# Looked-up embedding rows put in place by SyncE's on-chip transfers of 16-byte pieces instead of ScalarE's copies

## The reference

```python
e = stack([tbl_f[ids[:, f]] for f in range(39)], axis=1)          # (1024, 39, 16)
def cin_layer(x0, xk, W, b):
    out = einsum('bhd,bmd,shm->bsd', xk, x0, W) + b[None, :, None]
    return relu(out)
x1 = cin_layer(e, e, W1, b1)                                       # (1024, 128, 16)
x2 = cin_layer(e, x1, W2, b2)
z = concatenate([x1.sum(axis=-1), x2.sum(axis=-1)], axis=-1)
h = concatenate([z, dense_ctx], axis=1)
h = maximum(h @ W_top1 + b_top1, 0)
h = maximum(h @ W_top2 + b_top2, 0)
y = h @ W_top3
```

## Time and profile before

| | |
|---|---|
| timed runs, median of 3 (lowest, highest) | 1232.25 us (1232.1, 1232.55) |
| the profiled execution: its time, its span | 1228.31 us, 1226.4 us |
| granted TensorE clock, mean of the span | 0.992 |
| busy: TensorE, VectorE, ScalarE, GpSimd | 1172.4, 1005.4, 672.1, 864.8 us |
| DMA: software queue (look-ups), hardware queue (SyncE's loads) | 10240 and 2461 packets |

### The profile page before, as it was taken

How to read it: one execution, slowest core, us unless ns; L and a number is a source line. 1 busy time by engine, 2 the same in 40 slices (tenths; PEclk the granted TensorE clock), 3 DMA queues, 4 the chain that set the end, 5 groups by cost and what they waited for, 6 DMA issues and landing times.

```text
span 1226.4 us, 17749 instructions
## 1 busy us (share of the span) xinstructions
PE 1172.4 (96%) x4784; PEld 879.4 (72%) x4784; DVE 1005.4 (82%) x3692; ACT 672.1 (55%) x2188; POOL 864.8 (71%) x836
## 2 busy tenths in 40 slices
PE   3899999999999999999999999999999999999996
PEld 2577777777777777777776667777777777777775
DVE  4298898888899888888896678888888888887695
ACT  2656666665565656556564465555655565545430
POOL 7888878888888788788776757888886454444350
PEclk9899999999999999999999999999999999999997
DMA  5000000000000000000000000000000000000000
GB/s 177 5 4 4 4 4 3 4 4 5 3 4 3 4 3 3 4 4 3 4 4 3 3 3 3 4 3 4 3 4 2 1 1 1 1 1 1 1 1 1
DMA packets 12801, 9.08 MB, mean 7 GB/s; under 512 B 6190, under 2 KB 11822, under 8 KB 12573
## 3 DMA queue, kind: packets, MB, share of 16 engines
q0 software_dynamic: 10240, 2.64, 2.6%
q1 hardware_dynamic: 2461, 5.31, 1.3%
HBM read 7.92 MB, written 0.00 MB: 6 GB/s over the span
## 4 chain that ended last, share of the span: by engine, by line
PE 72%; DVE 18%; ACT 5%; issue 2%; POOL 2%; DMA 0%; SPq 0%; ACTq 0%
PE ps L724 17%; PE ps L726 17%; PE ps L725 17%; DVE acc L634 15%; PE ps L702 13%; PE ps L690 3%; PE ps L755 3%; ACT e L464 2%; ACT fy L425 2%; POOL looked L339 2%; DVE x1l L595 1%; PE ps L678 1%; DVE e_hl L580 1%; PE ps L697 0%; DVE e_hl L583 0%
## 5 line engine op out<-in xcount | busy, mean ns | idle before, releaser
L634 DVE SCALAR_TENSOR_TENSOR acc<-ps,e,acc 128x128 f32<-128x128 f32 x3200 | 854.4, 343 | 155.7 <-PE ps L726 152.4
L724 PE MATMUL ps<-w2h,x1h 128*128 128x512 f32 (+1 forms) x1280 | 582.4, 455 | 24.9 <-ACT fy L425 13.8
L348 POOL TENSOR_TENSOR fy<-fy 128x512 f32<-128x512 f32 (+1 forms) x256 | 403.0, 1574 | 214.3 <-ACT fy L425 193.5
L425 ACT ACTIVATE fy<-ps,e 128x128 f32<-128x128 f32 x1536 | 418.1, 387 | 198.8 <-PE ps L726 198.3
L726 PE MATMUL ps<-w2h,x1l 128*128 128x512 f32 (+1 forms) x1280 | 495.4, 387 | 0.0
L725 PE MATMUL ps<-w2l,x1h 128*128 128x512 f32 (+1 forms) x1280 | 494.3, 386 | 0.0
L339 POOL DMA_INDIRECT looked<-in_table,rows x320 | 310.9, 972 | 79.1 <-issue 55.0
L724 PEld LDWEIGHTS ps<-w2h,x1h 128*128 128x128 f32 x1280 | 241.5, 189 | 134.1 <-DVE acc L634 50.9
L725 PEld LDWEIGHTS ps<-w2l,x1h 128*128 128x128 f32 x1280 | 241.6, 189 | 82.6 <-issue 44.7
L726 PEld LDWEIGHTS ps<-w2h,x1l 128*128 128x128 f32 x1280 | 240.7, 188 | 48.4
L444 ACT ACTIVATE z<-ps 128x512 f32<-128x512 f32 x192 | 117.9, 614 | 224.8 <-PE ps L690 219.5
(11 more groups left out here) (64 smaller groups left out, 385.5 us busy)
## 6 DMA issues: line engine op xcount, KB each, us to landing
looked<-in_table,rows POOLq DMA_INDIRECT x320, 2.3
w_st<-in_w SPq DMA_DIRECT2D x1, 1728.0 KB, 10.2
wt_sb<-in_wt SPq DMA_DIRECT2D x2, 512.0 KB
w_st<-in_w SPq DMA_DIRECT2D x1, 768.0 KB, 6.3
w_sb<-in_w1a SPq DMA_DIRECT2D x1, 448.0 KB, 3.2
w1b_sb<-in_w1b SPq DMA_DIRECT2D x1, 448.0 KB, 3.8
sel_st<-in_sel SPq DMA_DIRECT2D x1, 234.0 KB
ids_sb<-in_ids SPq DMA_DIRECT2D x1, 150.0 KB, 4.9
```

The lines of the kernel that those rows point to most:

```text
L348: nc.gpsimd.tensor_tensor(out, a, b, ALU.add).then_inc(s_fsum, 1)
L425: nc.scalar.activation(fy[:, p % 2, sub, m - MD, :], ps[:, 2 * (nth % RING) + sub, k * S:(k + 1) * S], ACT.Copy, scale=emb(p, sub, m)).the ...
L634: nc.vector.scalar_tensor_tensor(acc[:, sub, :] if m < MD - 1 else y, y, emb(p, sub, m), acc[:, sub, :] if m else fsum[:, p % 2, sub, :], ...
L724: nc.tensor.matmul(y, x1h[:, t % 2, at], w2h[:, cols], start=True, stop=False)
```

## The change

From the third tile on, the 16 blocks of a tile are no longer copied by ScalarE but moved by 16 transfers that SyncE issues, SBUF to SBUF, as soon as that tile's look-ups have landed. A block has 32 partitions by 10 (or 9) fields by 4 numbers of 4 bytes: 320 (288) separate pieces of 16 bytes. Each tile has its own semaphore for them, `s_put[t - 2]`. The transfers go tile by tile, also where a fill takes two or four tiles; what reads `e` (`high_part`, `products`) waits for all tiles of its fill, and the look-ups of tile t + 8 for tile t's. The first two tiles stay as they were.

```diff
+PUT_DVE, PUT_ACT = (0, 1), (2, 3)
...
+        s_put = [sem(f"s_put{t}") for t in range(FIRST_TILES, TILES)]
...
+        def put_in_place(t, k, q):
+
+            return (e[q * BT:(q + 1) * BT, t, k:M:Q, :],
+                    looked[k * BT:(k + 1) * BT, t % LOOKED, 0:len(range(k, M, Q)), q * DT:(q + 1) * DT])
+
+        def wait_put(engine, t):
+
+            if t < FIRST_TILES:
+                engine.wait_ge(s_put_act, Q * len(PUT_ACT) * (t + 1))
+                engine.wait_ge(s_put_dve, Q * len(PUT_DVE) * (t + 1))
+            else:
+                engine.wait_ge(s_put[t - FIRST_TILES], 16 * Q * Q)
...
+                for t in range(FIRST_TILES, TILES):
+                    sp.wait_ge(s_look[t], 16 * LOOKUPS)
+                    for k in range(Q):
+                        for q in range(Q):
+                            sp.dma_start(*put_in_place(t, k, q)).then_inc(s_put[t - FIRST_TILES], 16)
                 sp.wait_ge(s_tail, 7)
...
-                        pool.wait_ge(s_put_act, puts_act(FILL_OF[t - LOOKED]))
-                        pool.wait_ge(s_put_dve, puts_dve(FILL_OF[t - LOOKED]))
+                        wait_put(pool, t - LOOKED)
...
                 def high_part(f):
                     tiles, at = filled(f)
-                    act.wait_ge(s_put_act, puts_act(f))
-                    act.wait_ge(s_put_dve, puts_dve(f))
+                    for t in range(tiles.start, tiles.stop):
+                        wait_put(act, t)
...
-                        if fill is not None and s in (1, 3, 4):
-                            put(fill, (1, 3, 4).index(s), 3)
...
                 def products(f):
 
                     tiles, at = filled(f)
-                    dve.wait_ge(s_put_act, puts_act(f))
-                    dve.wait_ge(s_put_dve, puts_dve(f))
+                    for t in range(tiles.start, tiles.stop):
+                        wait_put(dve, t)
```

More of the change, by code:

```diff
@@ L453, in first_layer, with put @@
                     nc.scalar.activation(x1[:, t % 2, :], ps[:, BK_ACC1, :], ACT.Relu, scale=0.5).then_inc(s_x1, 1)
[L455 to L464, removed]
+                def put(t):
+                    act.wait_ge(s_look[t], 16 * LOOKUPS)
+                    for k in PUT_ACT:
+                        for q in range(Q):
+                            nc.scalar.activation(*put_in_place(t, k, q), ACT.Copy).then_inc(s_put_act, 1)
                 def high_part(f):
                     tiles, at = filled(f)
-                    act.wait_ge(s_put_act, puts_act(f))
-                    act.wait_ge(s_put_dve, puts_dve(f))
+                    for t in range(tiles.start, tiles.stop):
+                        wait_put(act, t)
                     if tiles.start >= LOOKED:
@@ L504, in _ @@
                 nc.scalar.activation(wz[:], w1_sb[:, C1, :], ACT.Copy, scale=2.0).then_inc(s_wzh, 1)
-                put(0, 0, 1)
+                put(0)
                 high_part(0)
@@ L511, in _ @@
                 first_layer(0)
-                put(1, 0, 1)
+                put(1)
                 high_part(1)
@@ L556, in _, with put @@
             def _(dve):
-                def put(f):
-                    dve.wait_ge(s_look[f], 16 * LOOKUPS)
-                    for k in put_by_dve(f):
+                def put(t):
+                    dve.wait_ge(s_look[t], 16 * LOOKUPS)
+                    for k in PUT_DVE:
                         for q in range(Q):
-                            nc.vector.tensor_copy(*put_in_place(f, k, q)).then_inc(s_put_dve, 1)
+                            nc.vector.tensor_copy(*put_in_place(t, k, q)).then_inc(s_put_dve, 1)
                 def products(f):
                     tiles, at = filled(f)
-                    dve.wait_ge(s_put_act, puts_act(f))
-                    dve.wait_ge(s_put_dve, puts_dve(f))
+                    for t in range(tiles.start, tiles.stop):
+                        wait_put(dve, t)
                     if tiles.start >= LOOKED:
```

## The result

The changed kernel takes **1242.29 us** (median of 4 runs, 1241.72 to 1242.84); the kernel before took 1232.40 us (4 runs, 1232.10 to 1233.03) on the same chip. The ratio is 1.0080, 95% interval 1.0062 to 1.0097: **slower by 9.9 us**, where 1227.7 us was forecast and nothing above 1234.0 us was in the range. The profiled execution took 1241.88 us, its span 1240.1 us.

What follows compares the result with a forecast made beforehand. TensorE, busy 96%, was taken as the bound, with VectorE next; savings of 1.2 + 1.7 + 1.6 = 4.5 us in one-, two- and four-tile fills gave 1227.7 us, range 1222.0 to 1234.0.

Steps and rivals of the forecast that it cites:

- What bounds the kernel; removed: Whole loop: TensorE busy 96%, all fills cost 12.5 us; removing 240 ScalarE copies frees only TensorE's waits, VectorE limits next.
- One-tile fills: Tiles 2 to 7: TensorE starts 0.23 us earlier per fill, nothing at tile 2; 1.2 us in all.
- the ring of banks: TensorE's three banks in one-tile fills: a start 0.57 us earlier shrinks to 0.23 us, because VectorE's D bank ends at 104.76.
- the rule for L580 and L583: Fills: VectorE with two SBUF inputs and GpSimd lock shared ports for a whole instruction, so GpSimd's additions set VectorE.
- waits for no copies at all: One-tile fills: GpSimd said not to wait for ScalarE's copies, an argument against VectorE being set free as well.
- Two-tile fills: Six fills: 0.92 us saved is given back to VectorE; GpSimd, VectorE and TensorE come 0.29 us earlier, 1.7 us in all.
- a sign against itself: Two-tile fills: the forecast is wrong if L580's length moves by more than 0.1 us.
- Four-tile fills: Tiles 20, 24 and 28: gains of 0.5, about 0.1 and 1.0 us, 1.6 us in all.
- Added: the transfers: SyncE's 480 transfers: issue 7.5 and landing 1.8, 9.3 us a tile, leaving 6.7 us of cover at the tightest tile.
- B: Rival: transfers at 1.08 us each come late at tiles 2, 3, 8 and 9; slower, 1235.0 us; chance 0.16.
- A: Rival: GpSimd's additions get wholly out of VectorE's way in fills, giving the full 12.5 us: 1219.8 us; chance 0.08.
- C: Rival: TensorE's ScalarE waits become VectorE waits and GpSimd shifts cancel; saved 1.2 us or less, 1231.3 us; chance 0.21.

Runs made afterwards that it cites:

- e3: Changed kernel, with GpSimd waiting for VectorE's product before its last three additions in pairs with a fill: 1226.87 us, ratio 0.9998 to the kernel before.
- e2: Changed kernel, with ScalarE's copies put back in their old places but writing to a buffer nobody reads: 1227.09 us, ratio 0.9999 to the kernel before.
- e1: Changed kernel without its 480 transfers, e filled once at the start with other numbers: 1238.07 us, ratio 1.0088 to the kernel before.
- e8: Changed kernel, with GpSimd's waits and earlier fill places chosen per kind of fill, tile 28's without a wait: 1227.18 us, ratio 0.9956 to the kernel before.
- e4: Changed kernel, with GpSimd's last additions in pairs with a fill waiting for both of VectorE's low parts: 1240.20 us, ratio 1.0106 to the kernel before.

## Why the prediction was wrong

*What bounds the kernel; removed.* Right: TensorE's waits for ScalarE in the fills (13.3 us) went to nothing, tiles without a fill stayed, and VectorE took TensorE next. TensorE's waits for VectorE grew by 22.4 us, though, not by some.

*One-tile fills: the step that failed.* The prediction said that VectorE's part of a fill "stays", and walked the ring of banks with the earlier trace rows as fixed. It did not stay: the product went from 0.21 to 1.45 us, and the three together added 1.41 us. The 0.23 us that the walk gave to TensorE were right as a term, as 1.41 - 0.23 is the measured +1.17 within 0.01, and 0.20 - 0.23 is the -0.03 of e3. The warning stood in the trace: the product began 0.05 us before GpSimd's two additions, and ScalarE had finished the bank that releases those only 0.12 us before they began. The text had the rule for L580 and L583, where the trace showed the wait, and didn't ask it of the one instruction that had just escaped; of one-tile fills it said that GpSimd "waits for no copies at all", and e2, in which only ScalarE's copies come back, shows that it depends on them. e2 and e3 show this cause from two sides, and e1 excludes the transfers. The Trainium skill, SBUF — State Buffer, section on two separate sides, cited in the prediction, describes this lock between VectorE with two SBUF inputs and GpSimd; the trace agrees, a product stretched by 1.24 us beside an addition of 1.36 us (half of 2.72).

*Two-tile fills.* That TensorE's 0.92 us would be given back was right. The 0.29 us "earlier for all three" failed by the same step: before, GpSimd's additions began at 420.27, just after the product at 419.91 had ended; moved forward they fell upon it. Product, low rows and low products went from 0.28, 1.17 and 0.82 us to:

```profile
431.69 1.52 DVE L561 TENSOR_TENSOR prod<-e 128x120 f32<-128x120 f32 x1
...
435.21 0.51 DVE L571 TENSOR_TENSOR e_hl<-e,e_hl 128x312 f32<-128x312 f32 x1
435.64 0.82 DVE L574 TENSOR_TENSOR e_hl<-prod,e_hl 128x120 f32<-128x120 f32 x1
```

That is 2.27 to 2.85 us, +0.58, and the stretches say +0.58 (36.55, the mean of six, less 35.97). L571 at 0.51 us moved by 0.66, which the prediction had named as a sign against itself.

*Four-tile fills.* Tile 28, with no look-ups in the way, came as forecast (-0.92 for -1.0). Tile 20 gained twice the 0.5 taken: the low rows and low products went from 1.26 and 0.94 us to 0.80 and 0.40, free of the additions. Tile 24 has the failed step and one more: its product went from 0.39 to 1.63 us, +1.24; ScalarE's wait gone is worth some 0.9 (as in tile 28); that leaves +0.3, and measured were +1.79. The remaining 1.5 us are those that TensorE was busy longer, at a lower granted clock (below).

*Added: the transfers.* Right that they don't matter, though the issue was mis-sized. Tile 3's sixteen took 10.54 us, 0.66 us each with the gaps (0.62 without, the median of all 480), above the 0.47 taken and under the 0.89 from which it would have mattered; a transfer lands in 1.9 us for 1.8. Neither ScalarE's nor VectorE's part waited for one in the changed kernel, and e1 finds no cost.

```profile
91.13 10.54 SPq L326 DMA_DIRECT2D e<-looked  x16
```

*The rivals.* B, the only one on the slow side, was not what happened. A (the additions out of the way altogether) happened at tiles 20 and 28 alone. C (shifts that cancel) stopped at zero; it is what e3 shows, once the order is kept. (Its 1231.3 us goes with 1.0 us saved, not with the 1.2 named beside it.) The case that was missing is a release that lets another engine in front: its place (the product, 0.05 us ahead of the additions) and its price (about one addition, 1.24 us a fill) were to be had from the trace before. That the order would turn over was not; it could have been a rival with a price.

## What to carry to other kernels

Before taking time off an engine that isn't the bound, look at what it releases, and then at what starts just before the released instruction on the engine that is next in line to be the limit (here 0.05 us before in tile 3, 0.36 us in a two-tile fill), where the two share something: there the order can turn over, and the price here was nearly a whole instruction of the other. Where the order is to be kept, say so with a wait, put on the engine that has slack and no longer than its slack (e3 and e8 against e4); here a copy that seemed in the way was also the wait. A change that loses in one kind of tile and gains in another is best taken apart by kind: the differences added up to within the measurement.

## What was not expected of the hardware

- **Who wins is not to be read from the recorded starts.** The product was recorded 0.05 us ahead of the additions and took 0.21 us (before, e2); recorded 0.07 us ahead it took 1.45 (after, e1). What differs is the age of GpSimd's release, ScalarE's bank: 0.12 to 0.15 us against 1.33. In both, GpSimd had just ended a look-up, 0.01 to 0.02 us before. That GpSimd with nothing left to wait for reserves the ports sooner than its record says is an inference; how it does so stays open.
- **A stall of TensorE may cost more than itself.** At tile 24 TensorE stood 1.82 us, until 882.01, and the granted clock was 0.83 from 880 to 884 us and 0.74 from 884 to 888, after 1.00; the 512-wide matmuls lasted 0.63 us and followed each other every 0.43, where 0.40 and 0.23 are usual (some 3 us at the lower level, 1.2 GHz, then back at 2.4):

```profile
882.01 0.50 PE L715 MATMUL ps<-w2h,x1h 128*128 128x512 f32 x1 [1.82 <-DVE acc L625]
...
883.37 0.63 PE L716 MATMUL ps<-w2l,x1h 128*128 128x512 f32 x1
```
```profile
884.00:888.00 4.00, 4.00 (x16) 3.25 (x16) 3.97 (x17) 1.20 (x2) 3.37 (x6) 0.74 0.04 3
```

  TensorE's busy time in that tile is 36.18 us, 1.5 more than in tile 28's or a one-tile stretch. e1 has the same stretch with 36.16 us and clock 0.96, after a stall of 1.81 us. The stalls of 1.64 us (tile 3) and 1.71 us (a two-tile fill) left the clock at 1.00, and so did one of 1.91 us in e1's tile 2 (at 69.30 us; that stretch's clock is 1.00). So the length of the stall alone doesn't decide; that the stall brought the clock down at tile 24 is inferred from the order in time, and what else it takes stays open.
- **Small pieces cost issue time, but little.** Transfers of 288 to 320 pieces of 16 bytes inside SBUF: 0.62 us each (the median of 480) on SyncE's queue, where 16 to 128 pieces took 0.43 to 0.46. Their 157,440 added packets took 6% more of 16 engines' span, 7.5 ns each (0.06 x 16 x 1240 / 157440), under the 9.7 ns taken.
